# Starting the expert stage without a barrier: gathers of normalised rows alone, weights split later

## The chip, the cores and the metric

The kernel runs on one core of one Trainium2 chip. The metric is the device time of one execution in microseconds (us); the kernel before takes 1244.33 us (median of three runs, 1243.87 to 1245.32). The core has five engines that run side by side and meet at semaphores: TensorE (PE), VectorE (DVE), ScalarE (ACT), GpSimd (POOL) and SyncE (SP, which here only issues DMAs). Each engine works through its own list in order, so an instruction that waits holds up everything behind it on its engine.

## The reference, cut to what matters

```python
# x: 32 x 256 x 256 float32, context: 32 x 77 x 256
x = x + tanh(g_xattn) * cross_attention(layernorm(x), context)   # 16 heads of 16
z = layernorm(x).reshape(8192, 256)
shared = swiglu(z @ w_in.T) @ w_out.T          # hidden size 512
g = argmax(softmax(z @ wg.T + gb))             # one of 2 groups
p = softmax(experts of group g) * prob(g)      # 4 experts per group
topv, topi = top_k(p, 2)                       # 2 experts per token
h = swiglu(z @ w1.T)                           # one hidden layer for all experts
routed = sum over the 2 experts of topv * (h @ w2[expert].T)
out = x + tanh(g_ffn) * (shared + routed)
```

All products are made to float32 accuracy from two rounded parts (hi and lo): three matmuls for each product. So every weight must be "split": ACT copies it to the rounded type (hi) and a subtraction gives lo.

## The kernel before, in words

**First part (up to about 780 us).** 32 blocks of 256 tokens go through attention, the shared feed-forward ("ffn") and the router, software-pipelined. The function `phase_one` (line 50 on) writes one list `order` by hand, and every engine walks the same list and does its own share of each entry. Attention of block b, layer norm (`norm2`), transposition (`x2T`) and router logits come some steps ahead of the ffn. The ffn works on chunks of two blocks, 24 steps each: steps 0 to 15 are the input products (steps 4fc to 4fc+3 for hidden slice fc), 16 to 23 the output products, and step 16+fc needs the lo part `gl` of slice fc, which POOL makes after ACT's copy `gh`. SP stores normalised rows (`norm2`) and shared results (`res`, at steps 19 and 23) to the halves 0:D and D:2D of a DRAM table `y`.

**Route.** DVE runs a chain of 30 small instructions for each group of tokens (pieces 0 to 29; piece 17 makes the running counts `carry`, PE's `rank` at piece 20 uses them, the last makes `rec`). POOL then scatters one record of 16 bytes for each token (token number, two weights, a spare word) into a DRAM table `tab` (pieces 30 on), sorted by pair of experts. There are 9 routes; the last two (numbers 7 and 8) are of 4 tiles of 128 tokens. "tiles 0, 1, 2" after the last route turn the counts into the list of 76 tiles of 128 tokens: the last of them makes `ti` and `ei` (tile addresses, expert numbers).

**Between the parts.** Once `ti` is there and all 64 scatters have landed, SP reads the records of tile after tile (`records`, L391), 4 tiles to a chunk, 19 chunks. The semaphores for them are shared: `chunks(c)` gives chunk 0 and chunk 1 one each, and chunks 2 to 5 one together, so whoever waits for chunk 2 waits for the 16 records of chunks 2 to 5.

The expert weights w2 (16 pieces) and w1 (4 pieces) go through 6 staging slots in SBUF: `load_w(x)` on SP may fill a slot again when pieces x-6 have been split. In this kernel w2 is loaded and split during ffn chunk 14 ("split_w2"), w1 at the end. DVE does the lo part of three of four w2 pieces, POOL that of the fourth.

Then ACT, DVE and POOL wait for all stores (`yr`, `yn`) and all scatters: a barrier, since the buffers of the second part (`yt`, over attention's `af`, and `w1h`, ...) lie over those of the first.

**Second part.** For each chunk POOL gathers rows of `y` by token number (both halves at once, 4 gathers of 128 rows), PE transposes the normalised half (`trans`, L704), makes the hidden layer (`hidden`, L718, four slices of 12 matmuls) and the experts' products (`experts`, L736 and L739, one tile at a time), DVE adds them up, and POOL scatters the tile to the output. PE's order is hidden(0,0..3) with trans(1,0) and trans(1,1) among them, then for each chunk c and tile k: hidden(c+1,k), trans(c+2,k-1) for k of 1 and 2, experts(c,k). POOL's `hidden` makes `gl2`, and experts(c,0) waits for all four of its chunk. DVE's product `f2` of slice n waits for `gl2` of slice n-2.

Of the kernel before, what the change touches and what calls it, by code (L numbers as in the profile page):

```python
# [13 lines left out]
P = 128  # L14
# [5 lines left out]
NE = 8  # L20
# [10 lines left out]
MK0 = 19  # L31

# [19 lines left out]
def phase_one():  # L52

    order = []
    at = {"ffn": 0, "r": 0, "k": 0}
    logits = set()

    def route():
        r = at["r"]
        if r < len(ROUTES) and ROUTES[r][2] in logits:  # L60
# [7 lines left out]
    for i in range(NB + 4):  # L68
# [12 lines left out]
        put(i - 3, ((2, "bias", 0), (1, "attT", 0), (4, "proj", 0), (7, "norm2", 0), (10, "x2T", 0)))  # L81
# [8 lines left out]
        for slot in range(12):  # L90
# [12 lines left out]
            x = 12 * (i - NB - 2) + slot - 6  # L103
            if 0 <= x < 2 * NE:
                order.append(("split_w2", x, 0))
        if i == NB + 1:
            order.append(("load_w2", 0, 0))
# [6 lines left out]
    n, k = 0, 0  # L114
    while at["ffn"] < 24 * NCH:
# [14 lines left out]
    return order  # L130


def build(nc, A, out):
    ctx = ExitStack()
    with ctx:
        order = phase_one()
# [10 lines left out]

# [5 lines left out]
        y = nc.dram_tensor("y_dram", (NT + 1, 2 * D), F, kind="Internal").ap()  # L153
        tab = nc.dram_tensor("tab_dram", (NC * NT + NPAD * P, 4), F, kind="Internal").ap()
# [40 lines left out]
        af = sb("af", [P, 6272])  # L195
# [19 lines left out]
        sb = sbs(ph1)  # L215
        identb = sb("identb", [P, P], BF)
# [8 lines left out]
        winh = sb("winh", [P, 2, 1024], R)  # L225
        winl = sb("winl", [P, 2, 1024], R)
        woh = sb("woh", [P, 4, D], R)
        wol = sb("wol", [P, 4, D], R)
# [30 lines left out]
        aTl = carve(P, [2, S])  # L259
        x1 = sb("x1", [P, 5, 2, D])  # L260
        xn2 = sb("xn2", [P, 2, D])
# [6 lines left out]
        res = sb("res", [P, 2, 2, D])  # L268
        lgT = sb("lgT", [20, 512])
# [41 lines left out]
        yt = [af[:, 2048 * k:2048 * k + 2048].rearrange("p (t d) -> p t d", t=4) for k in range(2)]  # L311
# [3 lines left out]
        ei = af[0:1, 5920:5920 + 2 * NTILE].bitcast(I32).rearrange("p (t k) -> p t k", k=2)  # L315
# [7 lines left out]
        yt.append(sb("yt", [P, 4, 512]))  # L323
# [6 lines left out]
        gl2 = sb("gl2", [P, 2, 4, 512], R)  # L330
        ot = sb("ot", [P, 8, D])
# [6 lines left out]

        def w2_stage(x):
# [3 lines left out]
        def w1_stage(fc):  # L343
            h = 512 * ((2 * NE + fc) % 6)
            return stage[:, h:h + 512].rearrange("p (c k n) -> p c k n", c=2, k=2)

        def w1_part(w, fc):
            return w[:, :, :].rearrange("p c (k n) -> p c k n", k=2)[:, :, :, fc * P:(fc + 1) * P]


        def w_landed(x):
            return s[f"wb{x % 6}"], 16 * (x // 6 + 1) + (16 if x >= 2 * NE else 0)

        def w2_split(x):

            return (s["w2p"], x // 4 + 1) if x % 4 == 3 else (s["wl"], x - x // 4 + 1)


        def sync(e):
# [14 lines left out]
            def load_w(x):  # L374
                if x >= 6:
                    e.wait_ge(s["wh"], x - 5)
                    e.wait_ge(*w2_split(x - 6))
                if x < 2 * NE:
                    src = A["w2T"][x // 2].rearrange("(f p) d -> p f d", p=P)
                    e.dma_start(w2_stage(x), src[:, 2 * (x % 2):2 * (x % 2) + 2, :]).then_inc(s[f"wb{x % 6}"], 16)  # L380
                else:
                    f = (x - 2 * NE) * P
                    src = A["w1T"].rearrange("(c p) (k n) -> p c k n", p=P, k=2)
                    for c in range(2):
                        e.dma_start(w1_stage(x - 2 * NE)[:, c], src[:, c, :, f:f + P]).then_inc(s[f"wb{x % 6}"], 16)
# [8 lines left out]
            for stage_, b, k in order:  # L394
# [59 lines left out]
                elif stage_ == "weights":  # L454
# [4 lines left out]
                    e.dma_start(y[NT:NT + 1, :], res[0:1, 0, :, :].rearrange("p t d -> p (t d)")).then_inc(s["clr"], 16)  # L459
                elif stage_ == "clear":  # L460
# [3 lines left out]
                elif stage_ == "load_w2":  # L464
# [4 lines left out]
                elif stage_ == "split_w2":  # L469
# [7 lines left out]
                elif stage_ == "records":  # L477
                    for c in range(2, NG):
# [7 lines left out]
        def tensor(e):  # L486
# [210 lines left out]
            def trans(c, t2):  # L697
                bk, (sem, v) = take("B", "z", c, t2)
                e.wait_ge(sem, v)
                e.wait_ge(s[f"ly{c % 3}{t2}"], 32 * (c // 3 + 1))  # L700
# [6 lines left out]
            def hidden(c, fc):  # L707
                if fc == 0:
                    e.wait_ge(s["z2l"], 2 * c + 2)
                if c == 0:  # L710
                    e.wait_ge(s["wl"], 3 * NE // 2 + fc + 1)
# [10 lines left out]
            def experts(c, t):  # L722
                k = 4 * c + t
                if k == 0:
                    e.wait_ge(s["ei"], 2)
                    e.wait_ge(*w2_split(2 * NE - 2))
                    e.wait_ge(*w2_split(2 * NE - 1))
# [28 lines left out]
        def scalar(e):  # L756
            e.wait_ge(s["cst"], 16 * 7)
            e.activation(tg[:, 0:2], gx[:, :], ACT.Tanh).then_inc(s["tg"], 1)
            for stage_, b, k in order:
# [102 lines left out]
                elif stage_ == "split_w2":  # L862
                    fs = slice(2 * (b % 2), 2 * (b % 2) + 2)
                    if b == 0:
                        e.wait_ge(s["pj"], NB)
                    e.wait_ge(*w_landed(b))
                    e.activation(w2v[:, b // 2, fs, 0, :], w2_stage(b), ACT.Copy).then_inc(s["wh"], 1)
# [615 lines left out]
```

## Time and profile before

| | |
|---|---|
| runs shown | 1244.33 us (1243.87 to 1245.32) |
| profiled execution, own time | 1249.96 us |
| its span | 1248.2 us |
| mean granted clock of TensorE | 0.977 |
| PE busy | 1146.9 us, 92% of the span |
| DVE, ACT, POOL busy | 804.2, 498.9, 545.6 us |

Times inside the trace count from the start of the span. "Idle before" in square brackets is how long the engine sat idle ahead of that instruction, and what it waited for. The granted clock (PEclk) is TensorE's, as a share of full speed (2.4 GHz); 0.5 is 1.2 GHz.

### The profile page before, as it was taken

The page shows a single profiled execution, that of the slowest core. Times are in us where ns is not written, and L with a number is a line of the kernel's source. Part 1 is how long each engine was busy: PE and PEld are TensorE (multiplying, and loading weights), DVE is VectorE, ACT ScalarE, POOL GpSimd, SP SyncE. Part 2 cuts the span into 40 slices and gives each one's busy share as a digit, 9 for nine tenths or more (in the row PEclk, how much of TensorE's full clock was granted, in tenths as well). Part 3 has the DMA queues.
Part 4 walks back from the last instruction along what each step waited for, and adds up shares of the span by engine and source line. Part 5 has one row for each costly group of instructions (what it writes and reads, how often), then busy time and mean ns, then how long its engine had stood idle before and what let it go on. Part 6 is the DMA issues. An engine that isn't in the chain of part 4 may idle for free.

```text
span 1248.2 us, 22408 instructions
## 1 busy us (share of the span) xinstructions
PE 1146.9 (92%) x7487; PEld 913.9 (73%) x7487; DVE 804.2 (64%) x1771; ACT 498.9 (40%) x780; POOL 545.6 (44%) x658
## 2 busy tenths in 40 slices
PE   1788999999998999999999978599999999999997
PEld 0366777777776777777677756478888888888886
DVE  4455687676675776876677576256666666666665
ACT  3355555545545545555454442222222222222220
POOL 2122335235334244353352543456565565655543
PEclk9989999999999999999999988799999999999999
DMA  4877476647456555745555142422222221222200
GB/s 154 142 145 133 97 123 113 109 95 132 98 105 106 112 97 108 135 99 109 105 99 87 37 142 70 114 47 75 64 66 67 67 74 60 67 69 69 71 31 6
DMA packets 108260, 115.32 MB, mean 92 GB/s; under 512 B 36941, under 2 KB 88431, under 8 KB 108146
## 3 DMA queue, kind: packets, MB, share of 16 engines
q1 hardware_dynamic: 96374, 85.43, 35.6%
q0 software_dynamic: 11776, 28.46, 7.5%
q8 instruction: 64, 1.05, 0.4%
q14 instruction: 46, 0.38, 0.1%
HBM read 50.47 MB, written 28.64 MB: 63 GB/s over the span
## 4 chain that ended last, share of the span: by engine, by line
PE 72%; issue 9%; DVE 6%; POOL 4%; DMA 4%; ACT 2%; SPq 2%; POOLq 0%; another core or an unknown queue 0%; DVEq 0%; ACTq 0%
PE ps L718 16%; PE ps L736 11%; PE ps L636 9%; PE ps L739 6%; PE ps L653 5%; PE ps L544 4%; PE ps L556 4%; DMA w2a<-w2a 3%; PE ps L587 3%; PE ps L516 3%; PE ps L511 3%; PE ps L539 1%; POOL tab_dram L1390 1%; PE ps L565 1%; PE ps L610 1%
## 5 line engine op out<-in xcount | busy, mean ns | idle before, releaser
L736 PE MATMUL ps<-w2a,gh 128*128 x608 | 218.5, 398 | 0.0
L796 ACT ACTIVATE Pt<-ps,pbias 77x1024 f32<-77x1024 f32 x128 | 141.6, 1107 | 188.1 <-PE ps L544 178.4
L739 PE MATMUL ps<-w2a,gl 128*128 x608 | 171.0, 281 | 0.0
L1426 POOL DMA_INDIRECT out<-ot,Pt x76 | 78.6, 1034 | 151.6 <-DVE ot L1246 148.2
L736 PEld LDWEIGHTS ps<-w2a,gh 128*128 128x128 f32 x608 | 114.2, 188 | 24.5
L1105 DVE TENSOR_REDUCE mneg<-ps 128x8 f32<-128x616 f32 x128 | 101.5, 794 | 46.4 <-PE ps L516 44.4
L1366 POOL TENSOR_TENSOR x<-x,af 128x512 f32<-128x512 f32 x32 | 41.2, 1288 | 193.8 <-DMA x<-in_x 193.8
L718 PE MATMUL ps<-z2h,w1h 128*128 128x512 f32 x304 | 120.6, 397 | 5.5 <-DVE z2l L925 4.1
L894 ACT ACTIVATE tt<-ps 128x512 f32<-128x512 f32 x76 | 45.4, 598 | 197.4 <-PE ps L718 197.4
L718 PE MATMUL ps<-z2l,w1h 128*128 128x512 f32 x304 | 120.0, 395 | 0.0
L718 PE MATMUL ps<-z2h,w1l 128*128 128x512 f32 x304 | 120.0, 395 | 0.0
L739 PEld LDWEIGHTS ps<-w2a,gl 128*128 128x128 f32 x608 | 114.4, 188 | 1.5
L636 PE MATMUL ps<-x2h,winh 128*128 128x512 f32 x256 | 113.6, 444 | 0.8 <-DVE tt L1162 0.8
L1373 POOL TENSOR_TENSOR gl<-gf,gh 128x512 fp32r<-128x512 f32 x64 | 82.5, 1290 | 65.9 <-ACT gh L840 65.7
L1412 POOL TENSOR_TENSOR gl<-gf,gh 128x512 fp32r<-128x512 f32 x76 | 98.6, 1299 | 15.9 <-ACT gh L898 14.2
L636 PE MATMUL ps<-x2l,winh 128*128 128x512 f32 x256 | 103.0, 402 | 0.0
L636 PE MATMUL ps<-x2h,winl 128*128 128x512 f32 x256 | 102.9, 402 | 0.0
L898 ACT ACTIVATE gh<-gf 128x512 fp32r<-128x512 f32 x76 | 48.0, 632 | 123.2 <-DVE gf L1229 120.1
L1224 DVE SCALAR_TENSOR_TENSOR uu<-tt,ps 128x512 f32<-128x512 f32 x76 | 52.2, 687 | 62.6 <-ACT tt L894 62.6
L1310 POOL TENSOR_SCALAR ve<-mv 128x2 f32<-128x2 f32 x64 | 15.8, 247 | 175.5 <-DVE mv L921 175.0
L544 PE MATMUL ps<-w2a 100*77 100x256 f32 x512 | 89.4, 298 | 0.0
L1390 POOL DMA_INDIRECT tab_dram<-rec,slot x64 | 64.9, 1015 | 33.2 <-issue 13.9
(201 smaller groups left out, 2709.2 us busy)
## 6 DMA issues: line engine op xcount, KB each, us to landing
w2a<-w2a SPq DMA_DIRECT2D x96, 256.0 KB, 6.0
af<-in_x SPq DMA_DIRECT2D x32, 256.0 KB, 2.8
x<-in_x SPq DMA_DIRECT2D x32, 256.0 KB, 6.9
y_dram<-xn SPq DMA_DIRECT2D x32, 256.0 KB, 2.1
y_dram<-res SPq DMA_DIRECT2D x32, 256.0 KB, 2.1
w2a<-w2a SPq DMA_DIRECT2D x96, 77.0 KB, 4.8
Pt<-in_w2T SPq DMA_DIRECT2D x16, 256.0 KB, 3.6
af<-in_ctxT SPq DMA_DIRECT2D x16, 154.0 KB, 3.3
```

The source lines that it names most:

```text
L544: m = e.matmul(bk[0:K, j * S:(j + 1) * S], Kst[:, ks, j, p % 4, 2 * g + p // 4, :], Xs[:, h, p % 4, p // 4, :], start=False, stop=j == 1, ...
L636: m = e.matmul(bk[:, :], w[:, cc, off:off + P], x[:, b % 2, cc, :], start=cc == 0 and n == 0, stop=cc == 1 and n == 2)
L653: m = e.matmul(o[:, t, :], x[:, fc, at:at + P], w[:, fc, :], start=fc == 0 and t == 0 and n == 0, stop=fc == 3 and n == 2, skip_group_chec ...
L718: m = e.matmul(bk[:, :], w[:, cc, off:off + P], x[:, c % 2, cc, :], start=n == 0, stop=n == 5)
L736: e.matmul(o, gh2[:, c % 2, fc, t * P:(t + 1) * P], w2v[:, bass.ds(val, 1), fc, :, :].rearrange("p o h d -> p (o h) d"), start=fc == 0, st ...
L739: m = e.matmul(o[:, 0, :], gl2[:, c % 2, fc, t * P:(t + 1) * P], w2v[:, bass.ds(val, 1), fc, 0, :].rearrange("p o d -> p (o d)"), start=Fa ...
L796: e.activation(Pt[0:K, 4 * k:4 * k + 4, :].rearrange("k (n j) t -> k n (j t)", n=2), bank_of["sc", b, k][0:K, :, :], ACT.Exp, bias=pbias[: ...
L1105: e.tensor_reduce(mneg[:, h, t, :].rearrange("p (j q c) -> p c j q", j=2, c=2)[:, c], bank_of["mm", b, k][:, :, 0:4 * K].rearrange("p q (f ...
L1373: e.tensor_tensor(gl[:, fc - 1, :], gf[:, n % 2, :], gh[:, fc - 1, :].bitcast(F), ALU.subtract).then_inc(s["gl"], 1)
L1390: e.indirect_dma_start(tab, bass.IndirectOffsetOnAxis(ap=slot[:, j:j + 1], axis=0), rec[:, j, :], None, bounds_check=NC * NT - 1, oob_is_e ...
L1412: e.tensor_tensor(gl2[:, c % 2, fc, :], gf2[:, fc % 2, :], gh2[:, c % 2, fc, :].bitcast(F), ALU.subtract).then_inc(s["gl2"], 1)
L1426: e.indirect_dma_start(out.rearrange("b s d -> (b s) d"), bass.IndirectOffsetOnAxis(ap=rt[:, k, 0:1].bitcast(I32), axis=0), ot[:, k % 8, : ...
```

## The change

The barrier ahead of the second part goes. The buffers are laid out anew, so that what is written first in the second part lies over what attention used. Weights: w1 comes first (pieces 0 to 3, in "split" entries during ffn chunk 14, steps 7 to 9), then ten w2 pieces (4 to 13) in ffn chunk 15, one entry after each of steps 0 to 9, behind the last route and "tiles"; the last six (14 to 19) are split among hidden(0,*) of the second part. DVE makes all lo parts, POOL none. The list of entries for the last block is drawn tighter (proj, norm2, x2T, logits earlier), the scatters of route 7 are held back until the root of the last layer norm is issued on POOL, and one round of 12 slots falls away (`range(NB + 3)`). The gathers of chunks 0 and 1 come in two: first the normalised half of the rows (through a view `y2` of twice as many rows, and a second token index in the record's spare word), later the result half (`gather_res`). The first four gathers stand behind ffn steps 10 to 13 of chunk 15, the next four at its end. The result halves and the four gathers of chunk 2 go, one of each, behind POOL's hidden(0,0), hidden(0,1), ... At the start of the kernel the result half of the last four blocks is written with zeros (4 more stores of 256 KB), and the record prefill gets one more memset.

```diff
-    for i in range(NB + 4):
+    for i in range(NB + 3):
...
-        put(i - 3, ((2, "bias", 0), (1, "attT", 0), (4, "proj", 0), (7, "norm2", 0), (10, "x2T", 0)))
+        put(i - 3, ((2, "bias", 0), (1, "attT", 0), (4, "proj", 0), (7, "norm2", 0), (10, "x2T", 0)) if i < NB + 2 else
+            ((1, "bias", 0), (1, "attT", 0), (3, "proj", 0), (5, "norm2", 0), (7, "x2T", 0), (9, "logits", 0), (10, "logitsT", 0)))
...
+            if i == NB + 2 and slot == 4:
+                held = None
+
+            if i == NB + 2 and 5 <= slot < 9:
+                order.append(("split", slot - 5, 0))
...
+            elif k == 3 and w < 14:
+                order.append(("split", w, 0))
+                w += 1
+            elif k == 3 and g < 4:
+                order.append(("gather", 0, g))
+                g += 1
...
-    order.append(("gather", 0, 0))
+    order += [("gather", x // 4, x % 4) for x in range(g, 8)]
     order.append(("records", 0, 0))
...
         def sync(e):
...
                     e.dma_start(y[NT:NT + 1, :], res[0:1, 0, :, :].rearrange("p t d -> p (t d)")).then_inc(s["clr"], 16)
+
+                    for n in range(NB - 4, NB):
+                        e.dma_start(y[n * S:(n + 1) * S, D:2 * D].rearrange("(t p) d -> p t d", p=P), res[:, 0, :, :]).then_inc(
+                            s["clr"], 16)
...
-                elif stage_ == "split_w2":
+                elif stage_ == "split":
                     if b + 6 < 2 * NE + 4:
                         load_w(b + 6)
                 elif stage_ == "tiles" and k == 2:
                     e.wait_ge(s["ti"], 1)
                     e.wait_ge(s["scat"], 16 * (NT // P))
                     records(0)
                     records(1)
                 elif stage_ == "records":
-                    for c in range(2, NG):
+                    records(2)
+                    for x in left:
+                        if x + 6 < 2 * NE + 4:
+                            load_w(x + 6)
+                    for c in range(3, NG):
                         records(c)
...
+                elif stage_ == "split":
+                    split(b)
...
-            e.wait_ge(s["gl"], 4 * NCH)
-            e.wait_ge(s["yr0"], 16 * NCH)
-            e.wait_ge(s["yr1"], 16 * NCH)
-            e.wait_ge(s["yn0"], 16 * NCH)
-            e.wait_ge(s["yn1"], 16 * NCH)
-            e.wait_ge(s["scat"], 16 * (NT // P))
...
                         hidden(c + 1, k)
+                    if c == -1:
+                        for x in left[3 * k:3 * k + 3] if k < 3 else left[9:]:
+                            split(x)
...
         def gpsimd(e)
+            def gather_z(c, t):
+                e.indirect_dma_start(yt[c][:, t, 0:D], None, y2,
+                                     bass.IndirectOffsetOnAxis(ap=rt[:, 4 * c + t, 3:4].bitcast(I32), axis=0),
+                                     bounds_check=2 * NT + 1, oob_is_err=True).then_inc(s[f"zz{c}{t // 2}"], 16)
...
-            e.wait_ge(s["res"], NB)
-            e.wait_ge(*chunks(2))
-            for t in range(4):
-                gather(2, t)
             for c in range(-1, NG):
                 for t in range(4):
                     if c + 1 < NG:
                         hidden(c + 1, t)
+                    if c < 1:
+                        if t == 0:
+                            e.wait_ge(s["ix"], c + 2)
+                        gather_res(c + 1, t)
+                    if c == -1:
+                        if t == 0:
+                            e.wait_ge(s["res"], NB)
+                            e.wait_ge(*chunks(2))
+                        gather(2, t)
```

`gather_res(0, 0)` waits for all `yr` stores, and so does DVE's first `experts`.

## Rows read from the trace of the kernel before

**Rows 1.** The page, part 1: busy time, share of the span, instructions of each engine.
```profile
PE 1146.9 (92%) x7487; PEld 913.9 (73%) x7487; DVE 804.2 (64%) x1771; ACT 498.9 (40%) x780; POOL 545.6 (44%) x658
```
**Rows 2.** PE's waits between 700 and 860 us: us in total, times, longest.
```profile
PE ps L704 <- DMA af<-y_dram,Pt: 11.5, 2, 9.7
...
PE ps L667 <- DVE carry L1009: 4.7, 2, 4.3
```
**Rows 3.** Windows of 4 us: busy of each engine, PEclk, DMA share, GB/s.
```profile
796.00:800.00 4.00, 4.00 (x10) 3.08 (x10) 2.05 (x4) 0.99 (x2) 0.00 (x0) 0.50 0.29 76
...
820.00:824.00 4.00, 4.00 (x21) 3.38 (x21) 2.39 (x5) 0.76 (x2) 1.91 (x2) 1.00 0.07 2
```
**Rows 4.** Timeline: start, duration, instruction; the last block's projection, norm and transposition.
```profile
727.34 0.75 DVE L1134 SCALAR_TENSOR_TENSOR x<-ps,tg,x 128x512 f32<-128x512 f32 x1
...
735.01 2.52 DVE L1144 TENSOR_SCALAR xn<-x,mv,rs 128x256 f32<-128x256 f32 x2 [4.69 <-POOL rs L1312]
...
737.68 1.09 PE L597 MATMUL ps<-ident,xn 128*128 128x128 f32 x4 [6.26 <-DVE xn L1144]
```
**Rows 5.** Timeline of DVE, an earlier block's norm.
```profile
670.82 0.73 DVE L1144 TENSOR_SCALAR xn<-x,mv,rs 128x256 f32<-128x256 f32 x2
```
**Rows 6.** Timeline: transposed logits, DVE's first use of them, the end of the route.
```profile
745.52 1.06 PE L621 MATMUL ps<-fold,lgT 20*128 20x10 f32 x8
749.80 0.15 DVE L1155 COPY LGg<-ps 128x8 f32<-128x8 f32 x1
...
764.41 0.22 DVE L1052 TENSOR_REDUCE rec<-cmp 128x8 f32<-128x64 f32 x1
```
**Rows 7.** Timeline of SP: record reads (L391) and stores (L452).
```profile
772.71 8.55 SPq L391 DMA_DIRECT2D Pt<-tab_dram  x8
781.31 0.94 SPq L452 DMA_DIRECT2D y_dram<-res  x2
783.30 46.22 SPq L391 DMA_DIRECT2D Pt<-tab_dram  x40
```
**Rows 8.** The line L380 (loads of w2): issue to landing.
```profile
DMA to landing us min/median/max: 2.6/3.6/5.8
```
**Rows 9.** Timeline: one or more splits on ACT (L867) and DVE (L1195), ACT's gh.
```profile
729.64 0.68 DVE L1195 TENSOR_TENSOR w2a<-Pt,w2a 128x512 fp32r<-128x512 f32 x1
...
752.85 1.66 ACT L867 ACTIVATE w2a<-Pt 128x512 fp32r<-128x512 f32 x3
...
774.77 0.63 ACT L840 ACTIVATE gh<-gf 128x512 fp32r<-128x512 f32 x1 [1.04 <-DVE gf L1170]
```
**Rows 10.** Timeline of POOL: a scatter, gl, a gather, the first gather of chunk 2.
```profile
730.37 0.97 POOL L1390 DMA_INDIRECT tab_dram<-rec,slot  x1 [0.30 <-issue]
...
773.81 1.29 POOL L1373 TENSOR_TENSOR gl<-gf,gh 128x512 fp32r<-128x512 f32 x1 [0.79 <-ACT gh L840]
...
791.85 1.01 POOL L1301 DMA_INDIRECT af<-y_dram,Pt  x1 [0.31 <-issue]
...
805.12 1.01 POOL L1301 DMA_INDIRECT yt<-y_dram,Pt  x1 [9.63 <-DMA Pt<-tab_dram]
```
**Rows 11.** The chain that ended last: start, duration; two ffn output steps and the last five.
```profile
706.54 1.42 PE ps L653 x12
...
776.81 3.71 PE ps L653 x30
```
**Rows 12.** Timeline of PE in the second part: first hidden, a stall, trans of chunk 2.
```profile
795.62 0.80 PE L718 MATMUL ps<-z2h,w1h 128*128 128x512 f32 x1 [1.41 <-issue]
...
814.12 0.80 PE L718 MATMUL ps<-z2h,w1h 128*128 128x512 f32 x1 [4.06 <-DVE z2l L925]
...
824.08 0.60 PE L704 MATMUL ps<-ident,yt 128*128 128x128 f32 x4
```
**Rows 13.** The start: a window (columns as in rows 3) and a timeline row.
```profile
30.00:40.00 10.00, 3.59 (x15) 1.85 (x14) 7.56 (x10) 4.55 (x5) 0.00 (x0) 1.00 0.91 176
...
44.34 0.45 PE L539 MATMUL ps<-cauT,identb 77*77 77x154 bf16 x2 [2.83 <-DMA w2a<-w2a]
```

More of the change, by code:

```diff
@@ L31 @@
 MK0 = 19
+CLR = 16 * 9
 DCON = {n: i + 1 for i, n in enumerate(
@@ L55, in phase_one @@
     at = {"ffn": 0, "r": 0, "k": 0}
+    held = len(ROUTES) - 2
     logits = set()
@@ L59, in route @@
         r = at["r"]
-        if r < len(ROUTES) and ROUTES[r][2] in logits:
+        if r < len(ROUTES) and ROUTES[r][2] in logits and not (r == held and at["k"] >= R_SCAT):
             order.append(("route", r, at["k"]))
@@ L127, in phase_one @@
     order += [("tiles", 0, x) for x in range(k, 3)]
-    order.append(("gather", 0, 0))
+    order += [("gather", x // 4, x % 4) for x in range(g, 8)]
     order.append(("records", 0, 0))
-    return order
+    return order, list(range(w, 2 * NE + 4))
 def build(nc, A, out):
@@ L135, in build @@
     with ctx:
[L136 removed]
+        order, left = phase_one()
         names = (
@@ L259, in build @@
         aTl = carve(P, [2, S])
+        xn2 = sb("xn2", [P, 2, D])
+        lgT = sb("lgT", [20, 512])
+        res = sb("res", [P, 2, 2, D])
         x1 = sb("x1", [P, 5, 2, D])
-        xn2 = sb("xn2", [P, 2, D])
+        winh = sb("winh", [P, 2, 1024], R)
+        winl = sb("winl", [P, 2, 1024], R)
+        woh = sb("woh", [P, 4, D], R)
+        wol = sb("wol", [P, 4, D], R)
         x2h = sb("x2h", [P, 2, 2, 512], R)
@@ L322, in build @@
         w1l = sb("w1l", [P, 2, 1024], R)
-        yt.append(sb("yt", [P, 4, 512]))
+        yt = [sb(f"yt{k}", [P, 4, 512]) for k in range(3)]
+        ot = sb("ot", [P, 8, D])
+        gl2 = sb("gl2", [P, 2, 4, 512], R)
         z2h = sb("z2h", [P, 2, 2, 512], R)
@@ L758, in scalar, with split @@
             e.activation(tg[:, 0:2], gx[:, :], ACT.Tanh).then_inc(s["tg"], 1)
+            def split(x):
+                e.wait_ge(*w_landed(x))
+                if x < 4:
+                    e.activation(w1_part(w1h, x), w1_stage(x), ACT.Copy).then_inc(s["wh"], 1)
+                else:
+                    e.activation(w2_part(x, 0), w2_stage(x), ACT.Copy).then_inc(s["wh"], 1)
             for stage_, b, k in order:
@@ L898, in hidden @@
                 e.activation(gh2[:, c % 2, fc, :], gf2[:, fc % 2, :], ACT.Copy).then_inc(s["gh2"], 1)
-            w1(0)
             trans(0, 0)
             trans(0, 1)
-            for fc in range(1, 4):
-                w1(fc)
             for c in range(-1, NG):
@@ L1053, in route, with split @@
                 yield
+            def split(x):
+                e.wait_ge(s["wh"], x + 1)
+                if x < 4:
+                    i = e.tensor_tensor(w1_part(w1l, x), w1_stage(x), w1_part(w1h, x).bitcast(F), ALU.subtract)
+                else:
+                    i = e.tensor_tensor(w2_part(x, 1), w2_stage(x), w2_part(x, 0).bitcast(F), ALU.subtract)
+                i.then_inc(s["wl"], 1)
             nonlocal_count = [0]
@@ L1191, in vector @@
                         e.tensor_tensor(lo, src, hi.bitcast(F), ALU.subtract).then_inc(s["sl"], 1)
[L1192 to L1196 removed]
+                elif stage_ == "split":
+                    split(b)
                 elif stage_ == "tiles":
                     tiles(e, k)
[L1201 to L1210 removed]
             def trans(c, t2):
@@ L1247, in experts @@
                                            ALU.mult, ALU.add).then_inc(s["acc1"], 1)
-            w1(0)
             trans(0, 0)
             trans(0, 1)
-            for fc in range(1, 4):
-                w1(fc)
             for c in range(-1, NG):
@@ L1257, in vector @@
                         hidden(c + 1, k)
+                    if c == -1:
+                        for x in left[3 * k:3 * k + 3] if k < 3 else left[9:]:
+                            split(x)
                     if c + 2 < NG and k in (1, 2):
@@ L1383, in gpsimd @@
                                channel_multiplier=1).then_inc(s["tok"], 1)
-                        e.wait_ge(s["tok"], b + 1)
+                        e.iota(rec[:, 0:J, 3:4].bitcast(I32), pattern=[[2 * P, J], [0, 1]], base=2 * t0 * P,
+                               channel_multiplier=2).then_inc(s["tok"], 1)
+                        e.wait_ge(s["tok"], 2 * b + 2)
                         e.wait_ge(s["rslot"], b + 1)
@@ L1413, in hidden @@
                                 ALU.subtract).then_inc(s["gl2"], 1)
-            e.wait_ge(s["res"], NB)
-            e.wait_ge(*chunks(2))
-            for t in range(4):
-                gather(2, t)
             for c in range(-1, NG):
```

123 lines of the change are left out of this document (52 added, 71 removed), and 4 rows, old and new, of the table names.

## The prediction

> **What bounds the kernel now.** I read the page's busy times first: PE is busy 92% of the span, the next engine 64% [rows 1], so the time can only come from PE's idle and slow stretches. The windows show the second part from 820 us on as PE without a gap at granted clock 1.00, and the seam between the parts as the place where it is not: 0.50 (1.2 GHz) after PE had stood still [rows 3]. PE's waits there name the holes: 6.26 us for the last block's norm [rows 4], 4.3 for the route's counts, 9.7 for the first gather behind the barrier [rows 2], and 4.06 in the middle of the first hidden layers [rows 12]. What follows trans(2,0), at 824.08 us, is the same PE work at full clock in both kernels, so the change is worth what it moves that instruction, plus what it does to the start.
>
> **The schedule of the new kernel, step by step.** I walk each engine's list with durations of before.
>
> Last norm. proj stands ahead of one pair of ffn steps, so DVE's L1134 comes one L1162 earlier, 727.34 - 0.5 = 726.85. POOL no longer puts scatters ahead of the root: statistics and root took 1.8 and 1.2 us, norm2 starts at 729.85 instead of 735.01. norm2 is 0.73 us alone [rows 5] and was 2.52 [rows 4] while POOL made a `gl` and a split; one `gl` is still beside it. I take 1.5 (0.7 to 2.5): done at 731.4, against 737.5. This is the real gain, 6.1 us, but four ffn steps that stood before the hole now stand behind it.
>
> Logits. From x2T to the transposed logits PE did 6.7 us of work in 8.9 (737.68 to 746.58) [rows 4, 6], the rest being clock. Now it is 5.3 us of work; with 1.9 for the clock (1.0 to 2.4) the transposed logits are done at 738.7.
>
> Route 8. DVE was 3.2 us late to them, and took 14.6 us from there to `rec` [rows 6], with two `res`, three splits (0.68 each) [rows 9] among them, and with small operations held up by POOL's splits. Without splits, and with what the list now puts between (two ffn products, one `res`, tiles 0), I count 12.4 us (11 to 14): `rec` at 751.1. PE waits about 2.5 us at the rank and 1.5 at tiles 2 instead of 4.3 and 1.2; all that is no matter, see below. From `rec` to SP's first record took 8.1 us (764.63 to 772.71: 4 scatters of 1.3 and their landing) [rows 6, 7, 10]; so SP has all scatters at 759.2 instead of 772.7. Up to here 13.5 us are won.
>
> **Where it is lost.** PE starts ffn chunk 15 at about 754 and would finish its 24 steps (0.7 us each, [rows 11]) by 771. But SP's list has "tiles 2" ahead of split 4, and the load of piece x+6 is issued at split x. So SP first waits for the scatters, then issues 8 records, 8.55 us [rows 7], and only at 767.8 the load of piece 10, 11 and 12 half a microsecond apart. Pieces 4 to 9 are in their slots; 10 is not. ACT and DVE meet split 10 after step 6, split 12 after step 8, and ACT's `gh` of slice 1 stands behind step 9. Loads of w2 take 2.6 to 5.8 us [rows 8]; with 4.2 for the third of them piece 12 is there at 773.0. Then ACT's split, tanh and copy, 0.55 + 0.6 + 0.63 [rows 9], 775.0 with hand-overs; POOL's `gl`, 1.3, 776.3. PE, which needs this `gl` at step 17, has been idle since about 765.
>
> POOL's list puts three gathers of 1.32 us [rows 10] ahead of the `gl` of slice 2 and the fourth ahead of slice 3: 776.3 + 4.0 + 1.3 + 1.3 + 1.3 = 784.2. PE then has five steps, 3.71 us at full clock [rows 11]; after such a hole the clock is 0.50 at first [rows 3]; I take 5.0 (3.7 to 7.0), 789.2 against 780.5. So the shared layer ends 9 us later than before although everything ahead of it was 13 us earlier.
>
> The `res` stores and the records go with it. From PE's last ffn step to SP's next record took 3.07 us (780.23 to 783.30), and from there the 16 records of chunks 2 to 5 took 21.8 us until POOL's gather of chunk 2 went at 805.12 [rows 7, 10, 11]. In the new kernel: 792.3 and 814.1.
>
> The z gathers (four of them early) do work: trans(0,0) follows the last ffn step at once, and hidden(0,0) starts at about 793 against 795.6, without the 9.7 us wait. PE makes hidden(0,*), trans(1,*), hidden(1,0), 15 us of work, and stands from about 810. For gather(2,0) is now behind POOL's hidden(0,0), and the `gl2` of slices 1 to 3 are behind gather(2,0), (2,1), (2,2) and as many result gathers. From 814.1: 1.32, gl2 1.3, 2.64, 1.3, 2.64, 1.3 = 10.5 us to the last `gl2`, 824.6. Before, the four gathers stood ahead of all four hiddens and cost one hole of 4.06 us [rows 12]. Then PE has ten matmuls of experts(0,0) and hidden(1,1), 1.75 + 2.8 us, at the low clock for its first microseconds: 6.5 (4.7 to 8). trans(2,0) at 831.1 instead of 824.1: **7.0 us later**. POOL keeps up behind that (5.3 us a tile against PE's 5.8 or so).
>
> Two side terms. The six last splits in hidden(0,*) are 0.68 us each on DVE [rows 9] in a stretch where DVE has half its time: nothing, covered by the wait for chunk 2; without it, up to 4.1 us. POOL's four splits are gone (5.2 us), beside a busy DVE. The extra iota of each route, 0.15 us nine times, hides in POOL's idle time.
>
> The start. Four more stores of 256 KB, issued in 2 us from about 35 us, when SP has 5 us to spare. But the DMA engines are 0.91 busy there [rows 13], and PE waits 2.83 us for a copy that leaves SP at 40.8 [rows 13]. At the 176 GB/s of that window [rows 13] 1.05 MB are 6.0 us; some of it delays that copy, and the first blocks are a chain with little to take the delay back. Bounds 0 and 6.0; I take 1.5, since by that rate the stores end at about 41 us, when the copy leaves.
>
> The Trainium skill (DMA: Bandwidth & Descriptors, the table of bandwidth per engine) gives each of 16 DMA engines some 27 GiB/s: by that the stores would be 2.3 us and this term an estimate of 0.6 or so; no row here shows such a rate.
>
> The traces have scatters 1.3 us apart beside DVE subtractions, such as at 729.64 and 730.37 [rows 9, 10], no slower than beside an idle DVE (1.32). [...]
>
> Sum: +7.0 + 1.5 = **+8.5 us**. The profiled execution (1249.96, span 1248.2) would become 1258.5 (1256.7), the median of the runs, 5.6 us below it, 1252.8. Adding the sizes that pull one way (norm 0.8, clock 1.0, route 1.4, landing 1.6, PE 1.3 and 1.8, the start 1.5) in squares gives 4 us down; upward, with 4.5 for the start and the upper ends given, 6. So the forecast's own range is 1249 to 1259.
>
> **The rivals.**
> 1. *Weights are in time, faster.* If the loads of pieces 10 to 12 don't hold ACT (SP gets through the records before ACT is at split 10), chunk 15 ends with PE's own work at 771, the next record goes at 774.1, those of chunks 2 to 5 are there at 795.9, the last gl2 at 806.4, trans(2,0) at 812.9, 11.2 earlier; with the start 1234.6. For it: 13.5 us are truly won ahead. Against: 8.55 us of records are measured, and it decides only if the scatters land by 752. 0.08. In a partial form the holes in chunk 15 are half as long (9 us less, by fewer instructions ahead of each `gl` than I count), 8.5 - 9 = about no change, 1240 to 1248: 0.12.
> 2. *Chunk 2 doesn't hold, faster.* If POOL's wait for chunk 2 were over when PE needs gl2, PE would run on from 793: 20.6 us of work and 2 of clock, trans(2,0) at 815.6, with the start 1237.3. Against: in the trace this very wait ended at 805.12, 21.8 us behind the first record [rows 7, 10]. 0.07.
> 3. *The zero stores hurt in full, slower still.* They delay the first blocks by 6.0 us and the seam's work runs 2 us longer at 0.50: 7.0 + 6.0 + 2 = 15, 1259.3. It decides if the DMA engines still have a queue at 40.8 us; 0.91 speaks for it, SP's 5 idle us against. 0.13.
>
> **Numbers.** Changes under 0.2%, 2.5 us, can't be told from none. Slower: the forecast 0.60 and rival 3, 0.13, less 0.02 of the forecast's low end, with 0.03 of the partial case: 0.74. Within 0.2%: 0.07. Faster: 0.08 + 0.07 + 0.04 of the partial case: 0.19. The range takes the forecast, the partial case and rival 3's middle: 1239 to 1260.
>
> **What would show it.** Right: in the new trace SP's loads of pieces 10 on come after eight records at about 768; ACT stands 3 us or more before a split; PE waits some 10 us ahead of an output step (L653) for `gl`; POOL's first gather of chunk 2 at about 814, and PE's largest wait of the second part ahead of L736 for gl2. Last scatter some 13 us earlier. Wrong: chunk 15 without holes, or the first gather of chunk 2 before 805; then the time falls. The start is judged by the first ffn product's time in both traces.

## The result, and the profile after

The changed kernel takes 1261.88 us (median of four runs, 1258.93 to 1262.86) against 1244.82 for the kernel before in the same series: a ratio of 1.0121, 95% interval 1.0082 to 1.0161, so 10 to 20 us slower. 8.5 us were forecast, with 1260 as the end of the range; the ratio times the 1244.33 us of the three runs shown ahead is 1259.4. In the profiled executions the span went from 1248.2 to 1259.7 us, 11.5 longer.

Where these 11.5 us lie is seen by two marks that both traces have: SP's issue of the last block's second load of x, and PE's trans(2,0). Between them PE does the same matmuls. SP's row of the first mark, and the window from mark to mark, first of before and then of after (columns of the windows as in [rows 3]):

```profile
719.47 0.47 SPq L443 DMA_DIRECT2D x<-in_x  x1
...
719.47:824.08 104.61, 73.13 (x347) 58.90 (x346) 57.69 (x129) 30.77 (x56) 45.25 (x43) 0.84 0.37 100
```
```profile
722.27 0.47 SPq L455 DMA_DIRECT2D x<-in_x  x1
...
722.27:835.53 113.26, 75.07 (x347) 60.93 (x347) 59.80 (x133) 30.20 (x56) 48.60 (x48) 0.80 0.32 88
```

I call this stretch the seam. It is 8.65 us longer, at a lower clock (0.80 against 0.84). The first part ends 2.8 us later, and what follows the seam is the same to 0.1 us (424.1 and 424.2). PE's waits of the changed kernel between 700 and 880 us (us in total, times, longest), against [rows 2] (9.7 for the first gather there):

```profile
PE ps L673 <- POOL gl L1402: 17.8, 3, 12.9
PE ps L758 <- POOL gl L1440: 6.5, 3, 3.2
PE ps L741 <- DVE z2l L941: 5.3, 2, 3.7
PE ps L617 <- DVE xn L1170: 4.6, 2, 2.5
PE ps L687 <- DVE carry L1025: 4.4, 1, 4.4
```

The wait behind the barrier is gone, and 17.8 us of waiting for `gl` of the last ffn chunk have come. SP's timeline shows why; against [rows 7]:

```profile
754.62 4.45 SPq L464 DMA_DIRECT2D y_dram<-res  x2
765.63 8.15 SPq L403 DMA_DIRECT2D Pt<-tab_dram  x8
773.90 10.16 SPq L393 DMA_DIRECT2D Pt<-in_w2T  x10
793.81 4.59 SPq L464 DMA_DIRECT2D y_dram<-res  x2
799.18 76.13 SPq L403 DMA_DIRECT2D Pt<-tab_dram  x68
```

The eight records (L403) start 7.1 us earlier than before, but the loads of weights (L393) stand behind them. The timelines of ACT, POOL and PE there:

```profile
776.65 0.63 ACT L788 ACTIVATE w2a<-Pt 128x512 fp32r<-128x512 f32 x1 [12.23 <-DMA Pt<-in_w2T]
...
780.10 0.63 ACT L788 ACTIVATE w2a<-Pt 128x512 fp32r<-128x512 f32 x1 [2.00 <-DMA Pt<-in_w2T]
...
781.81 1.27 POOL L1402 TENSOR_TENSOR gl<-gf,gh 128x512 fp32r<-128x512 f32 x1 [16.29 <-ACT gh L871]
...
783.13 0.58 PE L673 MATMUL ps<-woh,gh 128*128 128x256 f32 x1 [12.87 <-POOL gl L1402]
...
788.61 0.58 PE L673 MATMUL ps<-woh,gh 128*128 128x256 f32 x1 [3.83 <-POOL gl L1402]
...
791.34 0.58 PE L673 MATMUL ps<-woh,gh 128*128 128x256 f32 x1 [1.09 <-POOL gl L1402]
```

ACT stands 12.2 us before split 10 and again before split 12; POOL's `gl` of slice 1 and PE's output step follow. Behind it PE's first hidden(0,0), POOL at the first gather of chunk 2, and PE at experts(0,0) and trans(2,0), against [rows 10, 12]:

```profile
799.66 0.50 PE L741 MATMUL ps<-z2h,w1h 128*128 128x512 f32 x1 [1.57 <-DVE z2l L941]
...
818.55 1.01 POOL L1315 DMA_INDIRECT yt<-y_dram,Pt  x1 [11.50 <-DMA Pt<-tab_dram]
...
824.81 0.79 PE L758 MATMUL ps<-w2a,gh 128*128 x1 [3.18 <-POOL gl L1440]
828.60 0.79 PE L758 MATMUL ps<-w2a,gh 128*128 x1 [2.79 <-POOL gl L1440]
...
835.53 0.60 PE L727 MATMUL ps<-ident,yt 128*128 128x128 f32 x4
```

### The profile page after: what moved, and what is told of

The parts are those of the page before. It is cut to its first block, busy times and chain, and to the rows that moved or that the text cites. A ratio compares the mean times of both kernels' runs of the same rounds, so it can differ in the third digit from the quotient of the medians.

```text
span 1259.7 us, 22434 instructions
## 1 busy us (share of the span) xinstructions
PE 1148.4 (91%) x7487; PEld 916.4 (73%) x7487; DVE 805.2 (64%) x1776; ACT 497.8 (40%) x780; POOL 552.9 (44%) x673
## 4 chain that ended last, share of the span: by engine, by line
PE 66%; issue 13%; DVE 6%; POOL 6%; DMA 4%; ACT 2%; SPq 2%; POOLq 0%; DVEq 0%; ACTq 0%
PE ps L741 15%; PE ps L758 11%; PE ps L656 7%; PE ps L761 6%; PE ps L673 5%; PE ps L564 3%; DMA w2a<-w2a 3%; PE ps L576 3%; PE ps L607 3%; PE ps L536 2%; PE ps L531 2%; POOL tab_dram L1421 2%; PE ps L559 1%; PE ps L727 1%; PE ps L641 1%
## 5 line engine op out<-in xcount | busy, mean ns | idle before, releaser
L1131 DVE TENSOR_REDUCE mneg<-ps 128x8 f32<-128x616 f32 x128 | 101.5, 794 | 45.1 <-PE ps L536 45.0
L1440 POOL TENSOR_TENSOR gl<-gf,gh 128x512 fp32r<-128x512 f32 x76 | 98.7, 1299 | 18.9 <-ACT gh L914 17.1
L656 PE MATMUL ps<-x2h,winl 128*128 128x512 f32 x256 | 101.5, 396 | 0.0
L673 PE MATMUL ps<-woh,gh 128*128 128x256 f32 x256 | 79.1, 309 | 17.8 <-POOL gl L1402 17.8
```

What stands on the lines that cost most here:

```text
L656: m = e.matmul(bk[:, :], w[:, cc, off:off + P], x[:, b % 2, cc, :], start=cc == 0 and n == 0, stop=cc == 1 and n == 2)
L673: m = e.matmul(o[:, t, :], x[:, fc, at:at + P], w[:, fc, :], start=fc == 0 and t == 0 and n == 0, stop=fc == 3 and n == 2, skip_group_chec ...
L1131: e.tensor_reduce(mneg[:, h, t, :].rearrange("p (j q c) -> p c j q", j=2, c=2)[:, c], bank_of["mm", b, k][:, :, 0:4 * K].rearrange("p q (f ...
L1440: e.tensor_tensor(gl2[:, c % 2, fc, :], gf2[:, fc % 2, :], gh2[:, c % 2, fc, :].bitcast(F), ALU.subtract).then_inc(s["gl2"], 1)
```

## The experiments

The first part takes a few microseconds more or less from one execution to the next (the first mark of the changed kernel and of four variants with the same start lay between 722.27 and 727.19), so the seam's length is read beside the ratio to the kernel before. All ratios are of that kind; that of the changed kernel is 1.0121. The seam is given in two parts as well: A from the mark to PE's first hidden(0,0), B from there to trans(2,0).

| kernel | seam, us | A | B | ratio, 95% interval |
|---|---|---|---|---|
| before | 104.6 | 76.2 | 28.5 | 1 |
| changed | 113.3 | 77.4 | 35.9 | 1.0121 (1.0082 to 1.0161) |
| e1 loads first | 105.6 | 69.4 | 36.1 | 1.0019 (0.9994 to 1.0043) |
| e2 chunk 2 alone | 101.5 | 74.9 | 26.6 | 1.0014 (0.9994 to 1.0034) |
| e3 both | 94.0 | 67.4 | 26.6 | 0.9960 (0.9935 to 0.9985) |
| e4 zeros late | 112.5 | 76.7 | 35.8 | 1.0078 (1.0040 to 1.0115) |
| e5 before with zeros | 104.7 | 76.8 | 27.9 | 1.0026 (1.0006 to 1.0047) |
| e6 before, tight last block | 104.3 | 76.0 | 28.3 | 0.9994 (0.9978 to 1.0010) |
| e7 = e1 + e2 + e4 | 93.4 | 66.8 | 26.6 | 0.9925 (0.9898 to 0.9952) |
| e8 gathers behind gl | 94.1 | 65.2 | 28.9 | 0.9930 (0.9905 to 0.9954) |
| e9 splits spread | 90.8 | 66.2 | 24.6 | 0.9939 (0.9918 to 0.9960) |
| e10 chunk 2 last | 101.3 | 74.9 | 26.4 | 1.0054 (1.0038 to 1.0071) |

B repeats well among kernels that have the same lists there: 35.8 to 36.1 (changed, e1, e4), 26.6 three times (e2, e3, e7), 27.9 to 28.5 (before, e5, e6). A does not: in the four kernels with the changed kernel's lists in A (changed, e2, e4, e10) it is 74.9 to 77.4, and in the four that add e1's edit (e1, e3, e7, e9) 66.2 to 69.4. So a difference of 2 us in A between two single executions shows nothing by itself. By the means of these fours (76.0 and 67.5) e1's edit is worth 8.5 us, all in A.

**e1, the loads first.** In SP's part of the changed kernel:

```diff
                 elif stage_ == "split":
+                    if b == 8:
+                        e.wait_ge(s["ti"], 1)
+                        e.wait_ge(s["scat"], 16 * (NT // P))
+                        records(0)
+                        records(1)
                     if b + 6 < 2 * NE + 4:
                         load_w(b + 6)
-                elif stage_ == "tiles" and k == 2:
-                    e.wait_ge(s["ti"], 1)
...
```

> The changed kernel with one thing moved on SP: the records of chunks 0 and 1 (and their wait for the scatters) come behind the loads of pieces 10 to 13 instead of ahead of them. Theory A (ACT's 12.2 us wait at split 10 and PE's 12.9 us hole in ffn chunk 15 come from the eight records ahead of these loads): the wait and the hole go, chunk 15 ends near 782 instead of 797, the first gather of chunk 2 comes 19.4 us after the next record, near 805 instead of 818.6, and the kernel gets 13 to 14 us faster than the changed one, about 1247. Theory B (chunk 15 is slow because ten splits on ACT and DVE and four gathers on POOL stand in its way, wherever the loads are): holes of 8 us or more stay ahead of the output products and the gain is under 5 us.

ACT's wait at the splits falls from 12.2 to 2.2 us. SP and POOL in this kernel's timeline:

```profile
761.91 4.38 SPq L393 DMA_DIRECT2D Pt<-in_w2T  x4
771.22 8.53 SPq L403 DMA_DIRECT2D Pt<-tab_dram  x8
...
777.24 1.11 POOL L1321 DMA_INDIRECT yt<-y_dram,Pt  x1 [4.30 <-DMA Pt<-tab_dram]
```

The seam is 7.7 us shorter, the ratio 0.010 lower (12.7 us, with the scatter of both). The loads' place was the cause of ACT's wait, but not of the whole hole: PE still waits 10.1 us for `gl`, 8.4 in one piece, as theory B had said. POOL now stands 4.3 us at the first gather, for the records, with `gl` of slice 2 behind it and two more gathers. Theory A's 13 to 14 us were too many at this spot, B's "under 5" too few: the hole had two causes in series.

**e2, chunk 2 alone.**

```diff
...
-            k = min(c, 2) + (c > 5) + (c > 11)
-            return s[f"rc{k}"], 16 * 4 * (1, 1, 4, 6, 7)[k]
+            k = min(c, 3) + (c > 5) + (c > 11)
+            return s[f"rc{k}"], 16 * 4 * (1, 1, 1, 3, 6, 7)[k]
```

> The changed kernel with a semaphore of its own for the four records of chunk 2 (before: shared by the sixteen of chunks 2 to 5). Theory A (POOL's 11.5 us wait at the first gather of chunk 2, with hidden's gl2 queued behind it, is what holds PE's experts(0,0)): the gather goes at about 806 instead of 818.6, PE's waits for gl2 (6.5 us) and z2l (3.7) shrink to 3 us together, trans(2,0) comes near 824 instead of 835.5, gain 10 to 12 us, about 1250. Theory B (POOL has 8 gathers and 4 subtractions there, 15.7 us, and that alone holds PE): gain under 4 us.

POOL's first gather of chunk 2 no longer waits; PE's waits for `gl2` are gone. The seam is 11.7 us shorter, in the upper half of what A said. But only 9.3 of them lie behind hidden(0,0), where the edit acts; the other 2.4 lie ahead of it, within the scatter of part A:

```profile
799.84 0.50 PE L741 MATMUL ps<-z2h,w1h 128*128 128x512 f32 x1 [1.57 <-DVE z2l L941]
...
826.43 0.60 PE L727 MATMUL ps<-ident,yt 128*128 128x128 f32 x4
```

PE's two largest waits that remain, the first in ffn chunk 15, the second in the first hidden layers:

```profile
PE ps L673 <- POOL gl L1402: 16.5, 3, 11.6
PE ps L741 <- DVE z2l L941: 6.0, 2, 4.4
```

**e10, chunk 2 last.** The changed kernel; the wait is kept, its place on POOL is not:

```diff
-                    if c == -1:
-                        if t == 0:
-                            e.wait_ge(s["res"], NB)
-                            e.wait_ge(*chunks(2))
-                        gather(2, t)
+                    if c == -1 and t == 3:
+                        e.wait_ge(s["res"], NB)
+                        e.wait_ge(*chunks(2))
+                        for x in range(4):
+                            gather(2, x)
```

> The changed kernel with its four gathers of chunk 2, and the wait for the sixteen records, moved behind POOL's hidden(0,3). The wait itself stays and ends when it did (19.4 us behind the first of those records), nothing else is changed. Theory A (the wait costs because gl2 is queued behind it on POOL): PE's waits for gl2 go, experts(0,0) is on time, and the seam gets 8 to 11 us shorter than the changed kernel's 113.3. Theory B (what costs is that the rows of chunk 2 come late): trans(2,0) waits for the gather instead, gain under 4 us.

```profile
797.95 0.50 PE L741 MATMUL ps<-z2h,w1h 128*128 128x512 f32 x1 [1.57 <-DVE z2l L941]
...
819.29 1.01 POOL L1315 DMA_INDIRECT yt<-y_dram,Pt  x1 [0.30 <-issue]
...
824.32 0.63 PE L727 MATMUL ps<-ident,yt 128*128 128x128 f32 x4
```

The seam is 12.0 us shorter up to trans(2,0), 9.5 of them behind hidden(0,0) and 2.5 ahead of it, where this edit does nothing; 0.5 are given back before trans(2,1). The sixteen records are issued as in the changed kernel, but when POOL comes to the wait, at 819.29, it is over. e2 and e10 take away different things and win the same in part B (9.3 and 9.5 us), so it is the two together, a wait for sixteen records and `gl2` behind it, that cost 9.4 us. Theory A's 8 to 11 held.

**e3, both e1 and e2.**

> Both edits, e1's and e2's, in the changed kernel. Theory A: the two stalls lie one behind the other, so the gains add up but for what POOL's own work leaves: trans(2,0) near 810, gain 22 to 27 us against the changed kernel, about 1236, faster than the kernel before. Theory B: not more than the larger of the two alone.

The seam falls by 19.3 us, and 7.7 + 11.7 = 19.4. That these add up so closely is partly luck, since each of the two holds some of the scatter of part A. What is shown is that B is the same with both edits as with e2's alone (26.6), and with e1's alone as in the changed kernel (36.1 and 35.9): the two do not touch each other, about 8.5 us in A and 9.4 in B. The total is under what I gave (22 to 27), by what e1 had missed. By the ratio, 0.9960 (0.9935 to 0.9985), it is faster than the kernel before.

**e4, the zero stores late, and e5, the zero stores alone.** e4 stores two blocks of zeros instead of four, five blocks later; e5 adds the four stores to the kernel before.

```diff
-                    for n in range(NB - 4, NB):
-                        e.dma_start(y[n * S:(n + 1) * S, D:2 * D].rearrange("(t p) d -> p t d", p=P), res[:, 0, :, :]).then_inc(
-                            s["clr"], 16)
+                elif stage_ == "zero":
+                    e.dma_start(y[b * S:(b + 1) * S, D:2 * D].rearrange("(t p) d -> p t d", p=P), res[:, 0, :, :]).then_inc(
+                        s["clr"], 16)
...
+        if 5 <= i < 7:
+            order.append(("zero", NB + i - 7, 0))
```

> The changed kernel with the zero stores out of the start: two of 256 KB instead of four, and five blocks later (behind the table's prefill). Theory A (the start of the changed kernel lost 2.8 us by block 31 because the four stores stand in the DMA engines ahead of the first blocks' copies): the copy that PE waits for lands as before (2.8 us instead of 4.2), the last block's loads are back at the old times, gain 2 to 3 us. Theory B (such an early slip is taken up again, or came from elsewhere, as from the new places of the buffers): gain under 1 us.

> The kernel before with the four zero stores of 256 KB added at the start, and nothing else. Theory A (they cost the first blocks 1.5 to 3 us): the copy that PE waits for before its first scores lands later (PE's wait 4.2 us instead of 2.8), the kernel gets 1.5 to 3 us slower, ratio 1.001 to 1.0025. Theory B (the slip is taken up again before the seam): PE's early wait is longer but the ratio is within 0.0005 of 1.

PE's wait at the first scores, in the changed kernel, in e5 and in e7 (which has e4's edit), against 2.83 in [rows 13]:

```profile
45.85 0.45 PE L559 MATMUL ps<-cauT,identb 77*77 77x154 bf16 x2 [4.23 <-DMA w2a<-w2a]
```
```profile
46.17 0.45 PE L543 MATMUL ps<-cauT,identb 77*77 77x154 bf16 x2 [4.27 <-DMA w2a<-w2a]
```
```profile
44.68 0.45 PE L560 MATMUL ps<-cauT,identb 77*77 77x154 bf16 x2 [2.84 <-DMA w2a<-w2a]
```

In these two kernels the stores delay this copy by 1.4 us, nearly the 1.5 that I took; that is the low end. Over all twelve kernels the wait is 2.83 to 2.86 us in the six without the four early stores and 4.23 to 5.67 in the six with them, 1.9 more in the mean. The sign that the prediction named for the start, the first ffn product, in the kernel before and in the changed one:

```profile
112.65 0.48 PE L636 MATMUL ps<-x2h,winh 128*128 128x512 f32 x1
```
```profile
114.92 0.48 PE L656 MATMUL ps<-x2h,winh 128*128 128x512 f32 x1
```

It is 2.3 us later. It stands at 112.13 to 114.75 in the six kernels without the early stores (mean 113.3) and at 114.36 to 116.80 in the six with them (mean 115.6), so 2.3 us is also the difference of the means. In all the stores cost 3.2 us by e5 (0.7 to 5.9). e4's ratio is 0.0043 lower, about 5 us less the 0.8 in its seam, but its interval overlaps that of the changed kernel, so e4 by itself shows no gain. Whether the delay grows behind the first blocks is open: the first mark scatters too much in single executions (e5's lies at 718.05, before that of the kernel before; e9's, without the early stores, at 723.41 and e10's, with them, at 723.05).

**e6, the tight last block alone.** The entries of the last block and the held scatters of the change, in the kernel before.

```diff
-        put(i - 3, ((2, "bias", 0), (1, "attT", 0), (4, "proj", 0), (7, "norm2", 0), (10, "x2T", 0)))
+        put(i - 3, ((2, "bias", 0), (1, "attT", 0), (4, "proj", 0), (7, "norm2", 0), (10, "x2T", 0)) if i < NB + 2 else
+            ((1, "bias", 0), (1, "attT", 0), (3, "proj", 0), (5, "norm2", 0), (7, "x2T", 0), (9, "logits", 0), (10, "logitsT", 0)))
...
+            if i == NB + 2 and slot == 4:
+                held = None
...
```

> The kernel before with the tighter entries of the last block and the held scatters alone (w2 is still split during ffn chunk 14, the barrier stays). Theory A (the early norm is a true gain, but here the splits of DVE and POOL still stand in the route's way): PE's 6.3 us wait for the norm shrinks to 2 to 3 us, and the kernel gets 2 to 5 us faster. Theory B (the norm's hole only moves, since what follows waits for the splits): gain under 1 us.

PE's waits in this kernel:

```profile
PE ps L708 <- DMA af<-y_dram,Pt: 10.6, 2, 9.1
PE ps L671 <- DVE carry L1013: 6.6, 1, 6.6
PE ps L601 <- DVE xn L1148: 5.6, 2, 3.3
```

My theory A failed. The hole of the norm fell from 6.26 to 3.3 us, near what was expected, that at the rank grew from 4.3 to 6.6, and the seam is 0.3 us shorter. DVE has `rec` 5.7 us earlier after the mark (39.2 against 44.9) and SP its first record 2.2 us earlier, and still trans(0,0) stands where it stood (70.9 and 70.8 us after the mark): PE's chunk does not end earlier, and the barrier's gathers come behind that. That the splits on DVE take the gain back is what PE's waits for DVE suggest; no run takes them away in this kernel.

**e7, all three.** It adds e4's edit to e3; no further diff.

> The changed kernel with the loads ahead of the records (e1), chunk 2's own semaphore (e2) and the later, fewer zero stores (e4). If the three terms add up (7.7, 11.7 and 1.4 us at their places in the traces, of which e3 showed 19.3 for the first two): 20 to 21 us under the changed kernel, 1239 to 1241, 5 us (0.4%) faster than the kernel before. If they don't: not under e3 (ratio 0.996).

The ratio is 0.9925, 9 us (6 to 13) under the kernel before and 24 under the changed one, a little more than the sum. The seam (93.4) is e3's to 0.6 us, so the rest lies ahead of it, if there is a rest: the intervals of e3 and e7 overlap.

**e8, the first gathers behind the last gl.**

```diff
-            elif k == 3 and g < 4:
+            elif k == 3 and g < 4 and at["ffn"] >= 24 * NCH - 6:
```

> e7 with one more move: POOL's first four gathers stand behind ffn steps 17 to 20 of chunk 15 instead of 10 to 13, so behind its last gl. Theory A (with the loads in time, what holds the output products is POOL waiting for the records of chunk 0 with gl of slices 2 and 3 queued behind three gathers): PE's wait of 6.9 us for gl goes to under 2, trans(0,0) waits for its gathers for some 2 us instead, and the kernel gets 3 to 5 us faster than e7. Theory B (the splits hold ACT and DVE anyway): gain under 1 us.

```profile
PE ps L728 <- DMA yt<-y_dram,Pt: 4.8, 1, 4.8
...
PE ps L674 <- POOL gl L1403: 2.8, 3, 2.2
```

The wait for `gl` went from 8.0 to 2.8 us, and trans(0,1) waits 4.8 for its gathers instead of none; the seam is 0.8 longer. The rows can't come earlier than the records, the records not before the last scatter, so the wait only changed its name. Of the theories A was right on the cause of the wait and forgot what is late next; B's "under 1 us" came true, but not by the splits that it named.

**e9, the last splits spread.** In e7, on ACT and DVE:

```diff
-                    if c == -1:
-                        for x in left[3 * k:3 * k + 3] if k < 3 else left[9:]:
-                            split(x)
                     if c + 2 < NG and k in (1, 2):
                         trans(c + 2, k - 1)
+                    if c == -1:
+                        for x in left[2 * k:2 * k + 2]:
+                            split(x)
```

> e7 with the last six splits two at a time behind hidden(0,0), (0,1), (0,2) and behind the trans of the same step, instead of three at a time ahead of it. Theory A (with chunk 2's wait gone the six splits, which the prediction put at nothing only because that wait covered them, hold DVE's z2l of chunk 1): PE's 4.4 us wait for z2l falls to 2 or less and the seam gets 2 to 4 us shorter than e7's 93.3. Theory B (z2l waits for PE's own transposition or for ACT): no change, under 1 us.

```profile
723.41:814.21 90.80, 68.79 (x347) 56.27 (x346) 59.39 (x133) 30.12 (x56) 47.33 (x47) 0.91 0.40 109
```

PE's wait for z2l falls from 4.4 to 2.6 us and the seam by 2.6 us (2.0 of them in part B, where the edit acts), 13.8 us under that of the kernel before. The total is not better than e7's (0.9939 against 0.9925, intervals overlapping): a gain of 0.2% can't be told in so many runs. e7 and e9 are both faster than the kernel before.

## Why the prediction was right, point by point

The sign, the place and the mechanism were right; the size was 8.5 us against 11.5 in the traces and 15 (10 to 20) by the ratio. The forecast for the runs was 1252.8, and by the ratio it is 1259.4, so the range, up to 1260, held by 0.6 us only. The forecast's own range ended at 1259; the last microsecond was room for rival 3, which did not happen, so there is luck in the upper bound. One reason why the two profiled executions show less than the ratio is on record: that of the kernel before took 1249.96 us, 5.6 more than the median of its runs, and that of the changed kernel 1261.43, 0.5 less than its median. The prediction kept these 5.6 us between the profiled execution and the median for both kernels, but they belong to that one execution: in the eleven other kernels the profiled execution lay from 3.3 us below to 4.1 above the median of its runs, 0.1 above in the mean.

Of the signs that the prediction named, ACT's wait (12.2 us), PE's wait at an output step (12.9) and the loads behind eight records were there. POOL's first gather of chunk 2 came at 818.55 - 2.8 = 815.8, not 814. The last scatter was 10.1 us earlier, not 13.

In the steps below 2.8 us are taken off the changed kernel's times, as the later first part. The sum of the steps was off by less (1.65 us) than part A of the seam moves between executions of the same lists (2.5), so the small differences among them are readings of one execution.

- **Last norm.** Forecast done at 731.4; 732.59 + 1.56 - 2.8 = 731.35. It took 1.56 us beside one `gl`, as taken.
- **Logits.** 738.7; measured 741.66 - 2.8 = 738.9.
- **Route 8.** `rec` at 751.1; measured 753.8. This is the term most mis-sized, by 2.7 us; over the nine kernels with this route it was 1.0 to 2.7. I gave 12.4 us from the logits to `rec`; it took 14.9. Two of DVE's small operations stood behind POOL's `gl` (duration 1.27 instead of 0.16 us, 0.94 instead of 0.17), PE waited 4.44 us at the rank, not 2.5, then ran at half speed (granted clock 0.50 from 750 to 754 us), and DVE's `res` waited 1.9 us for it. I had POOL's splits in the sum as gone and left its `gl` out.
- **Scatters.** 8.1 us from `rec` to the first record; measured 9.0. One scatter took 1.83 us instead of 0.97.
- **Records, loads, split 12, gh, gl.** 17.1 us from the first record to the end of `gl` of slice 1; measured 783.08 - 765.63 = 17.45. e1 shows that SP's order is the cause of ACT's wait.
- **Three gathers between two gl.** 7.9 us; 791.29 - 783.08 = 8.2. That POOL's list holds PE here even with the loads in time is shown by e1, where the first of them also waits 4.3 us for the records, which the forecast did not need; e8 shows that it is these gathers.
- **Five output steps** at low clock: 5.0; 5.8 (791.29 to 797.06).
- **To the next record:** 3.07; 2.1. **Sixteen records:** 21.8; 799.18 to 818.55, 19.4. These two made up for most of what the route and the scatters had lost.
- **From there to trans(2,0):** 17.0; 835.53 - 818.55 = 17.0. e2 and e10 show its cause. Counted from hidden(0,0), which I had at about 793 and which came at 799.66 - 2.8 = 796.9, I gave 38.1 us and it took 35.9: one error hid part of the other.
- **The six last splits** at nothing while the wait for chunk 2 covers them, up to 4.1 without it: e9 puts them at 2.0 to 2.6 us when the cover is gone.
- **The start.** 1.5 us; the copy is late by 1.4 in this trace (1.4 to 2.8 in six), the first ffn product by 2.3, and e5 gives 3.2 (0.7 to 5.9) for the whole. This term too was taken too small.

The sum of the seam's steps was 7.0 and is 8.65: +3.6 to the first record, +0.35, +0.3, +0.8, -1.0, -2.4, with rounding.

Rivals 1 and 2 did not happen, but e1 and e2 built them, each with its own cause taken out. Rival 1 was given 11.2 us of seam for loads in time; e1 won none against before (105.6). Its trans(0,0) came 15.3 us later after the mark than the rival had it (66.8 against 51.5), and 10.1 of these are PE's waits for `gl`, behind POOL's wait for the records and its gathers. Rival 2, 8.5 us earlier than before, stands beside 101.5, 3.1 earlier: there I had left out the six splits; from hidden(0,0) to trans(2,0) e2 took 4.0 us more than I gave (26.6 against 22.6), about the 4.4 that PE waited for z2l. Rival 3 (15 us, of them 6.0 by a full delay of the zero stores) met the size of the runs' ratio by chance: the stores' share is 2.3 us at the first ffn product and 3.2 by e5, and 6.0 lies just outside e5's interval.

From the rows of before I had read that scatters beside DVE's subtractions are as fast as others, and in the new kernel I let POOL and DVE slow each other only at the norm. That reading did not carry: the subtraction at 729.64 [rows 9] began 0.55 us behind a scatter and was over when the scatter at 730.37 began. In the kernel before:

```profile
729.09 0.98 POOL L1390 DMA_INDIRECT tab_dram<-rec,slot  x1 [0.31 <-issue]
```

In the changed kernel a scatter began 0.02 us behind the first of two subtractions of DVE:

```profile
734.67 1.28 DVE L1075 TENSOR_TENSOR w1l<-Pt,w1h 128x512 fp32r<-128x512 f32 x2
734.69 1.61 POOL L1421 DMA_INDIRECT tab_dram<-rec,slot  x1 [0.81 <-POOL rec L1413]
```

It took 1.61 us instead of 0.97 [rows 10]. The other way round, the DVE operation that compares two columns began 0.04 us behind a `gl` of POOL:

```profile
744.47 1.29 POOL L1402 TENSOR_TENSOR gl<-gf,gh 128x512 fp32r<-128x512 f32 x1 [3.04 <-ACT gh L871]
744.51 1.27 DVE L983 TENSOR_TENSOR gm<-LGg 128x4 f32<-128x4 f32 x1
```

The Trainium skill (SBUF — State Buffer, "SBUF: two separate sides") says that when a DVE operation has two SBUF inputs and a GpSimd operation reads SBUF, whichever of them starts first holds the port pair that they share for its whole time. The trace agrees for these two: 4 elements a partition took as long as the 512 beside them. A scatter that had begun 0.27 us ahead of DVE's pair of subtractions took its usual 0.97 us, and it was the pair that took long, beside the `gl` that followed:

```profile
739.17 0.97 POOL L1421 DMA_INDIRECT tab_dram<-rec,slot  x1 [0.30 <-issue]
...
739.44 2.56 DVE L1075 TENSOR_TENSOR w1l<-Pt,w1h 128x512 fp32r<-128x512 f32 x2 [0.35 <-ACT w1h L786]
...
740.15 1.28 POOL L1402 TENSOR_TENSOR gl<-gf,gh 128x512 fp32r<-128x512 f32 x1
```

The pair took 2.56 us here and 1.28 at 734.67. The scatter of 1.83 us, at 758.78, ran beside three small conversions and a subtraction; which of them it waited for is not shown.

## What to carry to other kernels

A barrier that goes leaves its waits to single queues: before counting it as won, walk each in-order queue past the place, and look for what is issued late behind something that waits (here eight record reads ahead of weight loads, about 8.5 us, and a wait for sixteen records ahead of `gl2`, 9.4 us). A semaphore that several chunks share is a wait for the last of them. And a term set at nothing because another wait covers it comes back with its price when that wait is mended, as six splits did here (2.0 to 2.6 us). A gain far ahead of the place that waits may not reach it: the early norm alone was worth 0.3 us. And before two variants are compared by one trace each, split the stretch where the edit begins to act: 2.5 of the 12 us that e2 and e10 seemed to win lay ahead of the place where their edits act.

## What the runs showed of the hardware that was not expected

DVE operations of 0.16 and 0.17 us on 4 and 12 elements a partition took 1.27 and 0.94 us beside a GpSimd subtraction, and a scatter took 1.61 us instead of 0.97 when DVE's subtraction of two SBUF tensors had begun 0.02 us before it. The same start of the program led to a first part between 722.3 and 727.2 us long up to the same mark, in five profiled executions; the runs do not show from what. Four stores of 256 KB at the start made a copy land 1.4 to 2.8 us later in six kernels.
